# RWKV block: GpSimd mixes the feed-forward's rows of tiles 0 to 4, and VectorE's per-tile order is changed

## The reference, cut to what matters

```python
xa = ln(x); sx = shift(xa) - xa
xxx = tanh((xa + sx * maa_x) @ maa_w1)            # five low-rank mixes
xm = xa + sx * (maa_stack + xxx @ maa_w2)         # rows for k, w, v, r, g
w = exp(-exp(time_decay + tanh(xw @ td_w1) @ td_w2))
# r, k, v = xr @ Wr.T ...; g = silu(xg @ Wg.T); per head, for each step t:
#   out = r_t . (u * a + s);  s = a + w_t * s;  a = k_t v_t
x1 = x + (groupnorm(out) * g) @ Wo.T
xc = ln(x1); sx2 = shift(xc) - xc
rr = sigmoid((xc + sx2 * ffn_maa_r) @ Wfr.T)
kk = square(relu((xc + sx2 * ffn_maa_k) @ Wfk.T))
out = x1 + rr * (kk @ Wfv.T)
```

## Time and profile before

| | |
|---|---|
| runs | 985.55, 982.31, 985.37 us; median 985.37 |
| profiled execution | 983.59 us, span 981.8 us |
| busy over the span | TensorE 939.2, VectorE 589.0, ScalarE 463.0, GpSimd 413.6 us |
| RWKV block | from about 805 us to the end |
| granted TensorE clock | 0.998 over the span |

### The profile page before, as it was taken

How to read it: one execution, slowest core, us unless ns; L and a number is a source line. 1 busy time by engine, 2 the same in 40 slices (tenths; PEclk the granted TensorE clock), 3 DMA queues, 4 the chain that set the end, 5 groups by cost and what they waited for, 6 DMA issues and landing times.

```text
span 981.8 us, 21454 instructions
## 1 busy us (share of the span) xinstructions
PE 939.2 (96%) x8300; PEld 789.6 (80%) x8300; DVE 589.0 (60%) x974; ACT 463.0 (47%) x1026; POOL 413.6 (42%) x572
## 2 busy tenths in 40 slices
PE   6999999888999999999999999999999899999998
PEld 3777777875788888998897888998888788678776
DVE  4999986668534433344356433344426766999883
ACT  3777875157643333333334333333332434576565
POOL 2164343668465333332246443342422862344231
PEclk9999999999999999999999999999999999999999
DMA  8100000310011110111101110111100100000000
GB/s 278 57 23 2 2 2 22 116 55 1 1 55 50 54 54 21 37 54 48 54 7 55 49 54 22 48 43 48 54 22 18 44 11 1 1 2 6 13 6 22
DMA packets 24146, 37.13 MB, mean 38 GB/s; under 512 B 4432, under 2 KB 16528, under 8 KB 23824
## 3 DMA queue, kind: packets, MB, share of 16 engines
q1 hardware_dynamic: 24080, 36.23, 12.1%
HBM read 35.17 MB, written 1.05 MB: 37 GB/s over the span
## 4 chain that ended last, share of the span: by engine, by line
PE 70%; DVE 12%; POOL 8%; issue 5%; ACT 4%; DMA 1%; SPq 0%; DVEq 0%; POOLq 0%; ACTq 0%
PE ps L1293 18%; PE ps L790 12%; PE ps L1310 9%; PE ps L1352 6%; PE ps L1961 5%; PE ps L1328 4%; PE ps L892 2%; PE ps L1338 2%; POOL sb L839 2%; POOL sb L837 2%; DVE sb L2489 2%; DVE sb L656 1%; DVE sb L650 1%; PE ps L421 1%; PE ps L2039 1%
## 5 line engine op out<-in xcount | busy, mean ns | idle before, releaser
L837 POOL TENSOR_TENSOR sb<-sb 128x256 fp32r<-128x256 f32 (+1 forms) x128 | 101.7, 795 | 281.8 <-DMA sb<-in_heads_a 142.8
L1293 PE MATMUL ps<-sb 128*128 128x512 f32 x768 | 187.8, 396 | 1.0 <-issue 1.0
L1293 PEld LDWEIGHTS ps<-sb 128*128 128x128 f32 x768 | 139.5, 188 | 33.1 <-ACT sb L1426 3.1
L790 PE MATMUL ps<-sb 128*128 128x256 f32 x1152 | 148.9, 286 | 0.2 <-DVE sb L938 0.2
L790 PEld LDWEIGHTS ps<-sb 128*128 128x128 f32 x1152 | 141.4, 191 | 2.5 <-issue 0.6
L839 POOL TENSOR_TENSOR sb<-sb 128x256 fp32r<-128x256 f32 (+1 forms) x128 | 116.9, 914 | 10.1
L1523 DVE SCALAR_TENSOR_TENSOR sb<-ps,sb 128x512 fp32r<-128x512 f32 x64 | 45.1, 746 | 96.4 <-ACT sb L1459 96.4
L1310 PE MATMUL ps<-sb 128*128 128x256 f32 x768 | 99.2, 285 | 0.4 <-DVE sb L1491 0.4
L1503 DVE TENSOR_REDUCE sb<-ps 128x8 f32<-128x520 f32 x32 | 22.4, 700 | 126.6 <-PE ps L1328 126.6
L1310 PEld LDWEIGHTS ps<-sb 128*128 128x128 f32 x768 | 95.0, 191 | 3.0 <-issue 0.9
L1426 ACT ACTIVATE sb<-ps,sb 128x512 f32<-128x512 f32 x64 | 43.8, 685 | 107.8 <-PE ps L1293 107.7
(11 more groups left out here) (221 smaller groups left out, 1653.0 us busy)
## 6 DMA issues: line engine op xcount, KB each, us to landing
sb<-in_heads_a SPq DMA_DIRECT2D x32, 386.0 KB, 3.1
sb<-in_heads_c SPq DMA_DIRECT2D x16, 256.0 KB, 3.6
sb<-in_heads_b SPq DMA_DIRECT2D x32, 128.0 KB, 3.0
sb<-in_mlp_a SPq DMA_DIRECT2D x16, 128.5 KB, 2.1
sb<-in_mlp_b SPq DMA_DIRECT2D x16, 128.0 KB, 2.1
sb<-in_w_r SPq DMA_DIRECT2D x1, 2048.0 KB, 7.6
sb<-in_encT SPq DMA_DIRECT2D x1, 1024.0 KB, 7.3
sb<-in_ctx SPq DMA_DIRECT2D x1, 1024.0 KB, 7.2
```

The costliest lines, as they stand in the source:

```text
L790: last = pe.matmul(m.acc(t), lhsT[x], rhs[w], start=opens and n == 0, stop=False, skip_group_check=True)
L837: pool.tensor_tensor(high, src, one, ALU.mult).then_inc(*G.did(name + "_high", u))
L1293: last = pe.matmul(m.ps[u][:, c, :], m.w_parts[u][w][:, (KD * q + k) * P:(KD * q + k + 1) * P], rows[x][:, k, c * 512:(c + 1) * 512], star ...
```

## The change

For tiles 0 to 4 the token mix is no longer folded into the weights: GpSimd makes the mixed rows (`ffn_mix`, three operations: a difference of 128x256, a product of 128x512 and a sum of 128x512, each waiting for the one before) into a new buffer pair `xkr`, and `ffn_keys` and `ffn_receive` have two terms, the latter over all 128 rows at once. Tiles 5, 6 and 7 (`TWO_TERMS`) keep the folded weights, which now lie in buffers of their own. `ffn_rows` and `f_state` of the next tile wait for `xkr` in place of `kk_rr`. On VectorE `gate`, `attended` and `mix1` go ahead of `receive`, `mix2` ahead of `bonus` and `out_heads`, `group_sum` behind `lora_rows`; behind the loop `receive` of tile 7 goes ahead of `attended` of tile 6. On GpSimd `receive` waits for `scan1` instead of `scan0` (but for tile 7), and `gated` of the tile before stands ahead of it.

```diff
+TWO_TERMS = range(LAST - 2, TILES)
...
@@ rwkv_consts_gpsimd
-    pool.tensor_tensor(m.wr[:, W_FK, :, :], m.wr[:, W_FK, :, :], m.wfks, ALU.subtract)
-    pool.tensor_tensor(m.wr[:, W_FR, :, :], m.wr[:, W_FR, :, :], m.wfrs, ALU.subtract).then_inc(m.s_scaled, 1)
+    pool.tensor_tensor(m.wfk1, m.wr[:, W_FK, :, :], m.wfks, ALU.subtract)
+    pool.tensor_tensor(m.wfr1, m.wr[:, W_FR, :, :], m.wfrs, ALU.subtract).then_inc(m.s_scaled, 1)
@@ rwkv_tensor, ffn_keys
+        if i in TWO_TERMS:
...
+        pe.wait_ge(*done["xkr"].at(i))
         for e in range(KD):
             last = product(m.key_bank(i)[:, e * P:(e + 1) * P],
-                           [(wk[:, k, e * P:(e + 1) * P], m.xc[:, k, :, s:s + S]) for wk, _, k, s in ffn_parts])
+                           [(m.wr[:, W_FK, k, e * P:(e + 1) * P], m.xkr[i % 2][:, 0, k, :]) for k in range(KD)])
@@ rwkv_tensor, ffn_receive
+        product(m.receive_bank(i)[:, D:2 * D],
+                [(m.xkr[i % 2][:, 1, k, :], m.wr[:, W_FR, k, :]) for k in range(KD)]).then_inc(*done["kk_rr"].did(i))
@@ rwkv_scalar, ffn_rows (and f_state of rwkv_gpsimd)
-            act.wait_ge(*done["kk_rr"].at(i - 1))
+            act.wait_ge(*done["kk_rr" if i - 1 in TWO_TERMS else "xkr"].at(i - 1))
@@ rwkv_vector
         products0(slot - 5)
+        mix2(slot - 4)
         bonus(slot - 6)
         out_heads(slot - 6)
-        mix2(slot - 4)
...
         products1(slot - 5)
-        group_sum(slot - 6)
         shift(slot - 3)
         lora_rows(slot - 3)
+        group_sum(slot - 6)
...
         ffn(slot - 8)
-        if slot in (5, 6):
-            gate(slot - 4)
+        gate(slot - 4)
+        attended(slot - 6)
+        mix1(slot - 3)
         receive(slot - 5)
-        if slot not in (5, 6):
-            gate(slot - 4)
-        attended(slot - 6)
         close(slot - 8)
-        mix1(slot - 3)
...
     scan1(LAST)
+    receive(LAST)
     attended(LAST - 1)
-    receive(LAST)
@@ rwkv_gpsimd
+    def ffn_mix(i):
+        rows = m.xc[:, :, :, :].rearrange("p k b s -> p (k b) s")
+        pool.wait_ge(*done["xc"].at(i))
+        pool.wait_ge(*done["f_state"].at(i))
+        pool.tensor_tensor(m.sx2.rearrange("p k (b s) -> p (k b) s", b=2), rows[:, :, 0:S], rows[:, :, 1:S + 1],
+                           ALU.subtract).then_inc(*m.own_pool.did("sx2", i))
+        pool.wait_ge(*m.own_pool.at("sx2", i))
+        if i >= 2:
+            pool.wait_ge(*done["kk_rr"].at(i - 2))
...
+        pool.tensor_tensor(m.xkr[i % 2], bc(m.sx2, 1, [P, 2, KD, P]), bc(factors, 3, [P, 2, KD, P]), ALU.mult)\
+            .then_inc(*m.own_pool.did("sxf", i))
...
+        pool.tensor_tensor(mixed, mixed, bc(rows[:, :, 1:S + 1], 1, [P, 2, 4, S]), ALU.add)\
+            .then_inc(*done["xkr"].did(i))
...
     def receive(i):
         sc = m.sc[:, 0:m.vj, :]
-        pool.wait_ge(*done["scan0"].at(i))
+        pool.wait_ge(*done["scan0" if i == LAST else "scan1"].at(i))
...
         first(slot - 4)
+        gated(slot - 5)
         receive(slot - 4)
         f_state(slot - 6)
-        gated(slot - 5)
         bonus(slot - 3)
+        ffn_mix_early(slot - 6)
```

More of the change, by code:

```diff
@@ L1947, in rwkv_consts_gpsimd @@
     wide = lambda name, n: bc(m.cols(name), 2, [P, KD, n])
+    pool.tensor_tensor(m.headsum_u, bc(m.headsum[:, :], 1, [P, KD, P]), wide("u", P), ALU.mult)
     pool.tensor_tensor(m.wfks, m.wr[:, W_FK, :, :], wide("ffn_k", D), ALU.mult)
[L1949 to L1950 removed]
+    pool.tensor_tensor(m.wfrs, m.wr[:, W_FR, :, :], wide("ffn_r", D), ALU.mult).then_inc(m.s_scaled, 1)
     pool.wait_ge(m.s_scaled, 1)
[L1952 to L1953 removed]
+    pool.tensor_tensor(m.wfk1, m.wr[:, W_FK, :, :], m.wfks, ALU.subtract)
+    pool.tensor_tensor(m.wfr1, m.wr[:, W_FR, :, :], m.wfrs, ALU.subtract).then_inc(m.s_scaled, 1)
 def rwkv_tensor(pe, m, ph, rows_split, before):
@@ L2103, in turn_ffn @@
         last.then_inc(*done["f_turned"].did(i))
-    ffn_parts = [(m.wr[:, W_FK, :, :], m.wr[:, W_FR, :, :], k, 1) for k in range(KD)]\
-        + [(m.wfks, m.wfrs, k, 0) for k in range(KD)]
+    ffn_parts = [(m.wfk1, m.wfr1, k, 1) for k in range(KD)] + [(m.wfks, m.wfrs, k, 0) for k in range(KD)]
     @of_tile
     def ffn_keys(i):
-        pe.wait_ge(*done["xc"].at(i))
-        pe.wait_ge(*done["f_state"].at(i))
+        if i in TWO_TERMS:
+            pe.wait_ge(*done["xc"].at(i))
+            pe.wait_ge(*done["f_state"].at(i))
+            for e in range(KD):
+                last = product(m.key_bank(i)[:, e * P:(e + 1) * P],
+                               [(wk[:, k, e * P:(e + 1) * P], m.xc[:, k, :, s:s + S]) for wk, _, k, s in ffn_parts])
+            last.then_inc(*done["kk_raw"].did(i))
+            return
+        pe.wait_ge(*done["xkr"].at(i))
         for e in range(KD):
             last = product(m.key_bank(i)[:, e * P:(e + 1) * P],
-                           [(wk[:, k, e * P:(e + 1) * P], m.xc[:, k, :, s:s + S]) for wk, _, k, s in ffn_parts])
+                           [(m.wr[:, W_FK, k, e * P:(e + 1) * P], m.xkr[i % 2][:, 0, k, :]) for k in range(KD)])
         last.then_inc(*done["kk_raw"].did(i))
@@ L2122, in ffn_receive @@
             pe.wait_ge(*done["rr"].at(i - 1))
[L2123 to L2127, removed]
+        if i in TWO_TERMS:
+            for n, (_, wr, k, s) in enumerate(ffn_parts):
+                for b in range(2):
+                    last = pe.matmul(m.receive_bank(i)[b * S:(b + 1) * S, D:2 * D], m.xc[:, k, b, s:s + S], wr[:, k, :],
+                                     start=n == 0, stop=n == len(ffn_parts) - 1)
+            last.then_inc(*done["kk_rr"].did(i))
+            return
+        product(m.receive_bank(i)[:, D:2 * D],
+                [(m.xkr[i % 2][:, 1, k, :], m.wr[:, W_FR, k, :]) for k in range(KD)]).then_inc(*done["kk_rr"].did(i))
     @of_tile
@@ L2822, in build @@
             scaled(at, n) for at, n in ((0, D), (KD * D, D), (KD * 2 * D, P)))
+        late = [5136]
+        m.wfk1, m.wfr1 = cut(1, late, [KD, D]), cut(1, late, [KD, D])
+        m.xkr = [cut(1, late, [2, KD, P]), cut(0, [6528], [2, KD, P])]
+        m.sx2 = scaled(KD * (2 * D + 3 * P), P)
         m.xl = [scaled(at, P) for at in (KD * (2 * D + P), KD * (2 * D + 2 * P))]
@@ L2889, in build @@
         m.tile_done["kk_raw"] = Signal(m.done["ctx_ps"].sem, len(ITEMS))
+        m.tile_done["xkr"] = Signal(m.done["ctx"].sem, len(ITEMS))
         m.own_vec, m.own_act, m.own_pool = (Own(sem(n)) for n in ("vector_own", "scalar_own", "gpsimd_own"))
```

9 lines of the change are left out of this document (8 added, 1 removed).

## The result

The changed kernel takes 1002.85 us, the median of four runs (1001.61 to 1008.09), against 983.84 us for the kernel before (980.4 to 985.55): ratio of the runs 1.0206, 95% interval 1.0185 to 1.0227 (the medians alone give 1.0193). It is slower, and by over three times what was forecast. Its profiled execution took 1003.46 us. Two single runs of later kernels, of 1292 and 2257 us, lie far outside all others and are left out of their ratios (not of their medians, which they move by 0.1 us).

The account below looks back on a forecast made before the run. TensorE was taken to lead, VectorE 1.8 us behind; the ring's delays ate TensorE's saving. Slot terms summed to +5.9 us on 983.59, so 989.5, or 991.3 from the median; 990.5 was taken, range 984.5 to 996.

Parts of the forecast that it names:

- the ring: Loop's repeating chain mixes, mix1, ..., out_heads, center, keys, receive, project, next mixes: period from 18.76 to 19.95 us.
- two periods: Loop, from slot 5's project to mixes of tile 7: +1.2 us each, +2.4 together.
- slot 8, to products1 of tile 7: Loop's end: project +1.7 us later, then +0.4 as GpSimd's bonus falls on receive or close.
- behind the loop, to gather: After products1 of tile 7: gated ahead of receive +1.0 us, attended after receive +0.6.
- TensorE's part: ffn_keys 1.79 to 0.90 us, ffn_receive 1.88 to 0.94: 1.83 us saved per tile, nothing for tile 4.
- VectorE's ring: Mixes' end to out_heads takes 6.6 us against TensorE's 4.78: center waits 1.8, cancelling the 1.83 saved.
- GpSimd's part: ffn_mix, 3.1 us a tile: its sum waits out receive, then holds close, adding 1.2 us to the 6.6.
- the sign: Expected in the new profile: VectorE's five scans at 3.6 us.
- what would show it: Slots 5 to 7: period near 20 us, TensorE idle 2 to 3 us before center, close 1.2 late.
- The chain of the sum: Slot-by-slot addition of delays through loop and list behind it, together +5.9 us.
- The sum slips by: Rival, chance 0.20: close precedes GpSimd's sum, which runs beside products0; period 18.7 to 18.9, time 985.6 or 987.4 us.
- Faster: Rival, chance 0.13: four slots give back 1.83 us each, 976.3; or VectorE's 17.7 us work sets the period, 979.

Follow-up runs that it names:

- the run of the order alone: Changed kernel with all eight tiles on the folded weights, so ffn_mix never runs and only VectorE's and GpSimd's orders differ from the kernel before: 999.93 us, ratio 1.0174.
- the run with warm products: Changed kernel plus six unread 128x512 products between gather's first two products and its wait for receive, slots 5 to 8: 990.87 us, ratio 1.0081.

## Why the prediction was wrong

The direction and the ring were right, the size was not: +5.9 us was forecast and +19.9 came (spans 981.8 and 1001.7). The terms, in the order of the prediction (before; mixes of tile 4 ended at 871.50 before, and now starts at 870.69 and ends 1.5 later, at 872.2, of which 0.3 lie ahead of the block):

| to | forecast | measured |
|---|---|---|
| mixes of tile 4 | +0.25 | +0.7 |
| slot 5 | -0.2 in sum | -0.7 in sum |
| two periods | +2.4 | +10.1 (twice 23.83 for 18.76) |
| slot 8, to products1 of tile 7 | +2.1 | +3.3 |
| behind the loop, to gather | +1.6 | +6.5 |
| the rest | 0 | +0.6 |

**TensorE's part: right.** The products went as costed, and with a clock at full speed the saving shows (17.3 to 17.9 us a slot with VectorE's list of before).

**VectorE's ring: right.** receive, close, products0, mix2 and bonus between mix1 and out_heads hold center; the run of the order alone shows 1.37 + 0.42 = 1.8 us, the number of the prediction. The idle in front of gather and its releaser, receive, are there as well.

**GpSimd's part: right in sum, wrong in place.** The prediction has the sum come "when VectorE's receive has just started", to stand until receive ends and then hold close. It came 0.09 us ahead of receive and held that, with 1.17 us in place of the forecast's wait of 1.4 and more. For the ring it is one: without the low clock the period would be 23.83 - 4.3 = 19.5, forecast 19.95. The relief of the scans was larger than forecast: the five took 3.01 us in these slots, where 3.6 had been named as the sign. But so both delays fell into one wait of 2.32 us in front of gather, and none in front of center, where "what would show it" looked for 2 to 3. The order of GpSimd's and VectorE's operations hung on 0.1 us, which no sum made from rows of 0.1 us' accuracy could decide. That a GpSimd operation at work holds VectorE's whole is what the Trainium skill (SBUF — State Buffer, SBUF: two separate sides) says of the pair of ports that the two share, where both read SBUF and VectorE has two inputs there; receive's 2.43 us agree.

**The step that failed: TensorE's waits were priced at their own length.** The chain of the sum adds 1.8 and 1.2 us to a slot and takes every product at its duration of before. But a wait of 2.32 us was followed by some 10 us at half the clock in two slots and some 7 in the third. That is 4.3, 4.3 and 2.3 us, 10.9 of the 14.0 us by which +19.9 exceeds +5.9, read against the run with warm products, where the clock is full. The term was put at nothing. The rows ahead of the prediction have one wait of 1.02 us, behind which the 32 records took 3.81 us, at full clock. But the trace of the kernel before, which has 0.998 over the span, has two longer waits in busy stretches ahead of the block:

```profile
184.75 4.61 PE L892 MATMUL ps<-sb 128*128 128x512 f32 x12 [2.48 <-POOL sb L839]
...
213.44 1.09 PE L1644 MATMUL ps<-sb 128*128 128x128 f32 x8 [2.20 <-DVE sb L1818]
```

Behind the first the granted clock is 0.50 from 186 to 188, and 12 records take 4.61 us that take 2.98 elsewhere (at 764.52); behind the second it is 1.00. So a wait of over 2 us had a price in that trace that came in one case of two, and the prediction had neither the term nor a rival with it. The Trainium skill (TensorE: Matmul & The Clock Gate, A second HAM failure mode: psum-queue depth-cycling) has a bf16 kernel in which short idle times between groups of products make the clock swing between its levels. It agrees in kind with the rows here, and I didn't weigh it.

That 990.87, the time with warm products, is the forecast's 990.5 is luck. In that profiled run 1.3 us were won ahead of the block, the slots up to products1 of tile 7 cost 2.7 us, where the forecast had 4.3, and the way from there to gather 4.3, where it had 1.6.

**The end: mis-sized, +1.6 for +6.5.** Both steps that were named are there (gated ahead of receive, attended behind it), but the row to follow was the third one in GpSimd's list, the 128x4 copy behind the two, on which keys of tile 5 hangs: 2.51 us, and the products behind it at the low clock (3.75 us for 16 records, 1.8 of the 6.5). The three steps share the term out. From products1 of tile 7 to gather it takes 16.7 us with receive ahead of mix1, 12.8 with gated behind receive, 12.0 with attended ahead of receive too, and 10.4, as before the change, with tile 4 folded. So gated and what hangs on it were worth 3.9 us where the forecast had 1.0, attended 0.8 where it had 0.6, and the norm's root behind ffn_mix of tile 4, which it didn't have here, 1.6. Undoing these took 983.52 to 979.10.

**The rivals.** "The sum slips by" is real, as a period of 18.6 us. In three slots it needed a wait to bring it about; in the first slot with ffn_mix, which has no close, it came by itself: the sum started at 874.20, 0.46 us behind receive, and was done 2.32 us later, beside products0, and TensorE waited 0.47 us. (The rival's own terms, -1.2, +0.5, +2.0 and up to 0.3 for two periods, make 1.3 to 1.6, not the 2.0 that it adds.) "Faster" came true in another order of VectorE: with receive ahead of mix1 the relief of the scans (3.01 us for 4.15) and TensorE's 1.83 us both count, and the period ends at VectorE's own work, 17.6 us, where that rival had 17.7. The prediction saw neither that this relief needs GpSimd's new order and not VectorE's, nor that the mixing alone costs 0.8%.

## What to carry to other kernels

When an engine that sets the pace gets a new wait, price the wait at its length and then again at what the clock does behind it: read the granted clock by slot after any change that opens a gap in TensorE's stream, and look in the trace of before for waits of that length and what the clock did behind them. If products nobody reads, laid into a gap, make the kernel faster, the clock was the cost. And when a list is reordered, follow every step behind the moved one to whoever waits for it: the smallest, a 128x4 copy, was the dear one here, and of two moves that came in one change, on top of the mixing, GpSimd's order was worth 5.6 us and VectorE's cost 18.
